# A four-layer graph network on one core: VectorE instead of GpSimd prepares each tile's edge rows in layer 0

## The reference, cut to what matters

```python
edge_index = jnp.stack([src, dst])            # 53125 edges among 3125 nodes, 256 features
x = _layernorm(x + _L0_gnn_ref(x, edge_index, W0, b0))       # layer 0
x = _layernorm(x + _L1_gnn_ref(x, edge_index, edge_weight, ...))
x = _layernorm(x + _L2_gnn_ref(x, W, att, src, dst))         # attention over edges
x = _layernorm(x + _L3_gnn_ref(x, edge_weight, W3, b3, src, dst))

# layer 0
h = x @ W
deg = segment_sum(ones, col, n)               # with a self loop for each node
dinv = rsqrt(deg)
out = relu(segment_sum(h[row] * (dinv[row] * dinv[col])[:, None], col, n) + b)
```

## Time and profile before

| | |
|---|---|
| median of 3 runs | 1625.72 us |
| lowest and highest run | 1624.23 and 1640.36 us |
| profiled execution | 1645.24 us |
| its span, first to last instruction | 1643.4 us |
| mean granted PE clock in it | 0.956 of full speed |
| busy: PE, DVE, POOL, ACT | 88%, 71%, 62%, 30% of the span |
| from 120 to 470 us, the steps of layer 0: PE busy | 326.66 of 350.00 us, clock 0.98 |
| same stretch: DVE busy, POOL busy | 276.90 and 267.95 us |
| same stretch: DMA engines busy | 0.49 of the time, 158 GB/s |

### The profile page before, as it was taken

One profiled execution on the slowest core, in us unless ns is written; L12 is line 12 of the kernel. 1 busy time (PEld: TensorE's weight loads), 2 busy tenths in 40 slices (PEclk: granted clock), 3 DMA queues, 4 the chain that ended last, 5 costly groups with the idle time before them and its releaser, 6 DMA issues.

```text
span 1643.4 us, 36677 instructions
## 1 busy us (share of the span) xinstructions
PE 1449.5 (88%) x12043; PEld 1159.1 (71%) x12043; DVE 1162.6 (71%) x2964; ACT 488.1 (30%) x909; POOL 1015.8 (62%) x1015
## 2 busy tenths in 40 slices
PE   4768899999888999999588888888888879999998
PEld 4657687778676788888366566666666657888887
DVE  9787878778683343445499999999999969444443
ACT  0332122212210010102345555555555546100000
POOL 0147777777773655655477777777777720357674
PEclk9989999999999999999699999989999979999999
DMA  8974554455467555552244444444444432666652
GB/s 205 104 153 148 167 162 133 161 173 165 129 207 246 185 190 171 183 176 68 72 113 112 112 114 113 112 112 113 113 112 112 113 111 99 246 216 214 208 155 79
DMA packets 132297, 241.50 MB, mean 147 GB/s; under 512 B 70299, under 2 KB 94975, under 8 KB 125967
## 3 DMA queue, kind: packets, MB, share of 16 engines
q0 software_dynamic: 45024, 128.68, 28.4%
q1 hardware_dynamic: 87087, 110.47, 22.5%
HBM read 193.42 MB, written 50.96 MB: 149 GB/s over the span
## 4 chain that ended last, share of the span: by engine, by line
PE 33%; POOL 29%; issue 18%; DVE 8%; DMA 8%; ACT 1%; POOLq 1%; SPq 0%; DVEq 0%; ACTq 0%
POOL ring L725 16%; PE bank L1718 15%; POOL ring L674 10%; PE bank L1666 7%; DMA ring<-edge_rows,ring 2%; PE bank L1850 2%; DMA big<-rows_layer,big 2%; POOL big L678 2%; PE bank L1727 2%; DMA ring<-rows_layer,ring 1%; DMA ring<-attention_rows,work 1%; PE bank L1536 1%; POOL ring L645 1%; PE bank L1501 1%; PE bank L1618 1%
## 5 line engine op out<-in xcount | busy, mean ns | idle before, releaser
L725 POOL DMA_INDIRECT ring<-attention_rows,work x420 | 398.5, 949 | 149.6 <-issue 147.2
L678 POOL DMA_INDIRECT big<-rows_layer,big x304 | 289.7, 953 | 265.4 <-issue 242.1
L674 POOL DMA_INDIRECT ring<-rows_layer,ring x152 | 233.2, 1534 | 54.2 <-issue 52.5
L1850 PE MATMUL bank<-work,ring 128*65 128x48 f32 x3360 | 238.8, 232 | 8.5 <-ACT work L890 7.9
L1850 PEld LDWEIGHTS bank<-work,ring 128*65 128x65 f32 x3360 | 227.9, 147 | 17.1 <-ACT work L890 14.4
L890 ACT ACTIVATE work<-work 128x960 f32<-128x960 f32 x84 | 161.6, 1924 | 84.2 <-DVE work L1397 83.2
L1718 PE MATMUL bank<-big,ring 128*128 128x256 f32 x750 | 164.2, 379 | 0.0
L1718 PEld LDWEIGHTS bank<-big,ring 128*128 128x128 f32 x750 | 142.5, 190 | 19.5
L1718 PE MATMUL bank<-big 128*128 128x256 f32 x664 | 145.9, 379 | 0.0
L1666 PE MATMUL bank<-big 128*128 128x256 f32 x608 | 139.8, 384 | 6.7 <-DMA big<-rows_layer,big 6.6
L1718 PEld LDWEIGHTS bank<-big 128*128 128x128 f32 x664 | 126.1, 190 | 17.7 <-ACT big L914 0.4
(11 more groups left out here) (256 smaller groups left out, 2343.6 us busy)
## 6 DMA issues: line engine op xcount, KB each, us to landing
adjacency<-big SPq DMA_DIRECT2D x16, 1600.0 KB, 6.6
big<-adjacency SPq DMA_DIRECT2D x16, 1600.0 KB, 7.6
ring<-adjacency SPq DMA_DIRECT2D x16, 1600.0 KB, 7.4
ring<-attention_rows,work POOLq DMA_INDIRECT x420
rows_layer<-big SPq DMA_DIRECT2D x50, 128.0 KB, 2.4
edge_rows<-edge_list SPq DMA_DIRECT2D x1, 4983.0 KB
big<-rows_layer,big POOLq DMA_INDIRECT x304, 3.0
rows_layer<-big SPq DMA_DIRECT2D x5, 960.0 KB, 10.5
```

The lines of the kernel that those rows point to most:

```text
L674: G.indirect_dma_start(out=rows0[:, s, :], out_offset=None, in_=y0tab[:, :], in_offset=bass.IndirectOffsetOnAxis(ap=src_l0[j][:, c:c + 1], ...
L678: G.indirect_dma_start(out=rows1[:, s, :], out_offset=None, in_=(y1tab if q < 2 * LAYER else y3tab)[:, :], in_offset=bass.IndirectOffsetOn ...
L725: G.indirect_dma_start(out=rows[0:EP, s, c, 0:ZG], out_offset=None, in_=ztab[:, :], in_offset=bass.IndirectOffsetOnAxis(ap=idx[:, g, c:c + ...
L1850: ins = mm(sum_banks[k % 3][0:FH, h * WIN:(h + 1) * WIN], rows[0:EP, s, c, h * FH:(h + 1) * FH], prob[:, k % 2, c, h * WIN:(h + 1) * WIN], ...
```

## The change

`edge_rows` on POOL keeps only the indirect DMA. The two small copies and the step of the row numbers become `next_rows` on DVE, and the panel test with the addition to `CODE` becomes `codes_of_panel` on DVE. In a step, DVE runs both between the second and the third `add_weights`: the codes of tile i+1, and the row numbers of tile i+2. The first ones stand ahead of the loop. The buffers `cur2` and `panel1` go.

```diff
-            pool.sem_inc(c_next, 1)
-
-            def edge_rows(col, i):
+
+            def edge_rows(i):
                 pool.wait_ge(c_T, i + 1)
                 pool.wait_ge(c_next, i + 1)
                 pool.sem_inc(held, 1)
-                G.tensor_copy(cur1, cur[:, bass.ds(col, 1)]).then_inc(pool_col, 1)
-                G.tensor_copy(panel1, panel[:, bass.ds(col, 1)]).then_inc(pool_col, 1)
-                pool.wait_ge(pool_col, 3 * i + 2)
-                pool.sem_inc(held, 1)
                 G.indirect_dma_start(out=raw.rearrange("p e f -> p (e f)"), out_offset=None, in_=etab[:, :],
                                      in_offset=bass.IndirectOffsetOnAxis(ap=cur1[:, 0:1], axis=0)).then_inc(c_gath, 16)
-                G.tensor_scalar(cur2, cur1, float(P // GRAN), float(DEAD), ALU.add, ALU.min).then_inc(pool_col, 1)
-                pool.wait_ge(pool_col, 3 * i + 3)
-                pool.sem_inc(held, 1)
-                G.tensor_copy(cur[:, bass.ds(col, 1)], cur2).then_inc(c_next, 1)
-                pool.wait_ge(c_gath, i * 16 + 16)
-                pool.sem_inc(held, 1)
-                G.tensor_scalar(off, raw[:, :, PID].bitcast(I16), panel1[:, 0:1], 256.0, ALU.is_equal,
-                                ALU.mult).then_inc(c_off, 1)
-                pool.wait_ge(c_off, i + 1)
-                G.tensor_tensor(raw[:, :, CODE], raw[:, :, CODE], off, ALU.add).then_inc(c_raw, 1)
...
+            def next_rows(i, col, first=False):
+                if not first:
+                    dve.wait_ge(c_gath, 16 * i)
+                    dve.wait_ge(c_moved, i)
+                V.tensor_scalar(cur1, cur[:, bass.ds(col, 1)], 0.0, None, ALU.add).then_inc(c_next, 1)
+                dve.wait_ge(c_next, i + 1)
+                V.tensor_scalar(cur[:, bass.ds(col, 1)], cur1, float(P // GRAN), float(DEAD), ALU.add,
+                                ALU.min).then_inc(c_moved, 1)
+
+            def codes_of_panel(i, col, first=False):
+                if not first:
+                    dve.wait_ge(c_raw, i)
+                dve.wait_ge(c_gath, 16 * i + 16)
+                V.tensor_scalar(off, raw[:, :, PID].bitcast(I16), panel[:, bass.ds(col, 1)], 256.0, ALU.is_equal,
+                                ALU.mult).then_inc(c_off, 1)
+                dve.wait_ge(c_off, i + 1)
+                V.tensor_tensor(raw[:, :, CODE], raw[:, :, CODE], off, ALU.add).then_inc(c_raw, 1)
...
             V.tensor_scalar(cur[:], first_f[:], float(DEAD), None, ALU.min).then_inc(s_cur, 1)
+            dve.wait_ge(s_cur, 1)
+            next_rows(0, DENSE[0], first=True)
...
+                if t == NT - 2:
+                    dve.wait_ge(s_nswb, 1)
+                    codes_of_panel(0, DENSE[0], first=True)
...
+            next_rows(1, (DENSE[0] + (nswb <= 1) * (DENSE[1] - DENSE[0])).with_bounds(min_val=DENSE[0], max_val=DENSE[1]))
...
-                        for q in range(4):
+                        for q in range(2):
+                            add_weights(k, i, q, r)
+                        codes_of_panel(i + 1, tile_of(k, r, 1))
+                        next_rows(i + 2, tile_of(k, r, 2))
+                        for q in range(2, 4):
                             add_weights(k, i, q, r)
```

More of the change, by code:

```diff
@@ L305, in gnn_program @@
         cur1 = carve(NPAN, 1, dt=I32)
-        cur2 = carve(NPAN, 1, dt=I32)
-        panel1 = carve(NPAN, 1)
         carve = carver(ring)
@@ L356, in gnn_program @@
         rows_landed = [sem(f"rows_landed{s}") for s in range(2 * TEN)]
-        rel_ready, hot_made, chunk_done, pool_col = sem("rel_ready"), sem("hot_made"), sem("chunk_done"), sem("pool_col")
+        rel_ready, hot_made, chunk_done, c_moved = sem("rel_ready"), sem("hot_made"), sem("chunk_done"), sem("c_moved")
         ld_dst, ld_src, ld_ew, ld_dsti, ld_x, ld_wts = (sem(f"ld_{n}") for n in ("dst", "src", "ew", "dsti", "x", "wts"))
@@ L683, in _ @@
                 G.memset(aw[j], 0.0).then_inc(c_zero, 1)
-            edge_rows(DENSE[0], 0)
+            edge_rows(0)
             for k in range(ND):
-                this, following = DENSE[k], DENSE[min(k + 1, ND - 1)]
                 with pool.Fori(0, nswb) as r:
-                    edge_rows((this + (r >= nswb - 1) * (following - this)).with_bounds(min_val=this, max_val=following)
-                              if following > this else this, nswb * k + r + 1)
+                    edge_rows(nswb * k + r + 1)
                 if k == 0:
@@ L1094, in _, with tile_of @@
             V.tensor_copy(unsorted[:], epsc[:]).then_inc(s_wz, 1)
-            dve.wait_ge(s_nswb, 1)
             nswb = dve.value_load(nswb_i[0:1, 0:1], min_val=1, max_val=MOST)
+            def tile_of(k, r, ahead):
+                this, following, then = (DENSE[min(k + j, ND - 1)] for j in range(3))
+                if then == this:
+                    return this
+                tile = this + (r + ahead >= nswb) * (following - this)
+                if ahead > 1:
+                    tile = tile + (r + ahead >= 2 * nswb) * (then - following)
+                return tile.with_bounds(min_val=this, max_val=then)
+            next_rows(1, (DENSE[0] + (nswb <= 1) * (DENSE[1] - DENSE[0])).with_bounds(min_val=DENSE[0], max_val=DENSE[1]))
             def one_hot_lo(h):
```

## The result

The changed kernel takes 1623.32 us (median of 20 runs, 1619.39 to 1627.50) against 1633.22 us (20 runs, 1622.28 to 1647.91). The ratio is 0.9937, 95% interval 0.9918 to 0.9956: faster by 0.6%, some 10 us, where the prediction said 24 us and 1601. The three runs of the kernel before that the prediction had to go by had a median of 1625.72 us, 7.5 us under that of the twenty. Note the spreads: 26 us before, 8 us after.

The account below looks back on a forecast made before the run. PE was taken to lose 26.6 us in layer 0's steps to rows gathered late by POOL. 26.6 - 5.6 + 0.9 + 3.2 - 0.9 = 24.2 us off the median 1625.72 gave 1601 us, range 1589 to 1618.

Parts of the forecast that it names:

- layer 0's waits are no longer for it, I take the microseconds off the median as they are: Whole kernel: the 24.2 us worked out on the profiled execution come off the median 1625.72 us in full, giving 1601.5.
- recovered by POOL: Layer 0's fourteen steps: all 26.6 us lost to late rows come back once POOL sheds its arithmetic, before what DVE adds.
- The floor of 308.0 us: Layer 0's fourteen steps with nothing waiting: seven at 20.71 us and seven at 23.29 us, against 334.59 us profiled.
- A stuck last gather is harmless: Ten-chunk steps: a last gather caught by DVE's run ends at 17.4 us; PE needs that row only 20.9 us in.
- The rule that spoke against the change: DVE's addition to `CODE` would be blocked by POOL's gathers, up to 15 us more over 16 steps; left out of the sum.
- DVE's insertion: Between second and third `add_weights`: 1.1 us of added work, making PE 0.4 us later a step, 5.6 us over fourteen steps.
- Rival A: DVE becomes the delay, registers unhidden and gathers met, 1.0 to 1.3 us a step: 1613 us, chance 0.11.
- B: Ten-chunk steps: the stall moves with the gathers and still gates PE, 10.5 us less gain: 1612 us, chance 0.10.
- C: DVE waits for edge rows landing after 7 us or more, stopping the quads: 11 us slower, 1637 us, chance 0.05.
- the low end: Of the range, 1589 us: DVE's lower bound (2.8 us more) and some 4 us for step 1's lower floor.
- Step 0: First step of layer 0: scatter's wait of 1.44 us goes, less 0.5 us for the insertion, 0.9 us gained.
- Step 15: Last step of layer 0: scatter waits and slow last matmuls recovered, less 0.4 us, some 3.2 us gained.

Follow-up runs that it names:

- b2_unchanged: The kernel before, unchanged, profiled again as a second further execution with its own trace: 1636.98 us in total, fourteen steps of 321.81 us.
- b3_unchanged: The kernel before, unchanged, profiled a third further time with its own trace: 1636.51 us in total, fourteen steps of 325.59 us.
- executions of the table: Six profiled executions without edits: four of the kernel before (1645.24, 1643.40, 1636.98, 1636.51 us) and two of the changed kernel (1622.16, 1627.93 us).
- e5_rows_late_again: Changed kernel with the row numbers moved two `add_weights` later, run again beside the changed kernel on one chip: 1616.15 us, against 1623.79 us.
- e2_rows_late: Changed kernel with the row numbers moved two `add_weights` later: 1620.90 us, ratio 0.9906 to the kernel before.
- b1: The kernel before, unchanged, profiled again as a first further execution with its own trace: 1643.40 us in total, fourteen steps of 334.02 us.

## Why the prediction was wrong

The forecast was a gain of 24.2 us and 1601 us; measured are 9.9 us and 1623.32.

**The step that failed** is "layer 0's waits are no longer for it, I take the microseconds off the median as they are". It carries the first term, 26.6 us "recovered by POOL", from one execution over to the median. For that execution the sum was nearly right: 1645.24 - 24.2 = 1621.0 us, and the changed kernel's profiled execution took 1622.16. But that execution had the longest steps of the four traced: 334.59 against 321.81 us of the shortest. With the latter the same working gives 321.81 - 308.0 = 13.8 us. I had seen that the profiled execution was 19.5 us over the three runs' median and put no place to it; a part of the very loss that the change removes was in it. By the traces, b2_unchanged and b3_unchanged reach layer 1 some 8 to 11 us after the changed kernel's two executions of the table, which is about the gain that was timed. Of the 21.8 us between 1601.5 and 1623.32, this transfer is 14.3; the other 7.5 are the median of three runs, which lay that much under the median of twenty. The surplus of the profiled execution should have been asked for first: in layer 0, three ten-chunk steps of the same work took 28.8, 28.8 and 23.3 us, so executions could differ there.

**What held.** The direction, and the mechanism: POOL's gathers start with PE's scatter, PE waits for none of them in the steps, and POOL waits for PE before each block, up to 11.2 us. The floor of 308.0 us: 307.70 with DVE's part removed, in part by luck as said above. A stuck last gather is harmless: a last gather still took 6.78 us in step 1 of the changed kernel, and in five of the fourteen steps of the one with late row numbers (e5_rows_late_again), and PE did not wait for a row. Four times in the changed kernel it was the gather of the edge rows that was held, for 6.7 us. The rule that spoke against the change (DVE's addition blocked by gathers that run beside it) is not seen: the 17 additions took 571 to 592 ns, the one at 98.45 us with no gather beside it and the one at 224.25 us with a gather that had started 0.67 us before it, both 0.57 to 0.58 us.

**DVE's insertion** was put at 1.1 us and took 1.26 in the median of the steps, PE's loss at 0.4 us a step and was 0.57 (8.0 us in fourteen steps in place of 5.6). Smaller terms were mis-sized here: behind the addition alone about 0.3 us of register work (0.58 us to the next operation, 0.30 in e2_rows_late), where 0.25 us was assumed for the whole, and a panel test of 0.29 us, in five steps 0.39 or 0.40, in place of 0.227. It lies within the bounds given. Rival A asked for 1.0 to 1.3 us a step, so it did not come about. B and C did not either; no row or edge row is waited for in the steps. The edge rows took 6.3 us to land in the median and 16.0 at most, where the forecast had 3 to 6 and C was to cost from 7 us on; yet DVE waited for them only once, 0.47 us at 114 us in step 0. Step 1, which relates no tile, took 21.5 us at the full clock (e2_rows_late), 1.8 under the floor of the other ten-chunk steps, where the low end allowed for 4.

**The ends.** Step 0: 116.01 to 134.99 is 18.98 us, where it had been 20.78: 1.8 gained in place of 0.9. Step 15: from the last transposes to layer 1 46.05 us, where it had been 48.22: 2.2 gained in place of 3.2. There a wait of 1.67 us for rows of the last block stays. Ahead of step 0's transposes 0.6 us were lost (116.01 against 115.41), in place of 0.9; since that point lay anywhere from 115.4 to 117.6 us in the executions of the table, it is no measurement. Nor are the other two: in b1, b2 and b3 step 0 took 19.2 to 19.9 us, and the stretch behind the last transposes 45.7, 50.0 and 45.8 us. The sum for the first two traces is 18.9 + 1.8 + 2.2 - 0.6 = 22.3 us at the start of layer 1.

**What stays open.** The medians of the kernel before were 1633.2, 1637.4, 1627.7 and 1635.6 us in four sets of runs, and single runs went down to 1614.85. All four traced executions took 1636.5 us or more, over the median of the first set. No trace shows what layer 0's steps look like in a median run or in the fastest; that fewer gathers get stuck in them is likely and not shown. Nor is it shown what decides whether a gather is held.

## What to carry to other kernels

A profile is one execution. Where the runs of a kernel spread by more than the effect that is to be sized, trace several executions before a wait's length becomes a term of a sum, and ask in which stage the spread lies. Before work is moved off an engine to shorten its stalls, find out what the stalls are: six added waits did in this case about what moving six instructions did. Before two sums over the same steps are compared, check the granted clock in both. And price an operation that is inserted between two waits of an engine with its register work; here the same operations cost less where longer ones ran just before them.

## What the runs showed of the hardware

A POOL gather that meets DVE's run of bf16 operations on SBUF, issued back to back, can be held until the run ends: 6.79 us, over some seven operations of about 1 us, not until the end of the one that is running. With waits added between these operations, it was let through within 2 us (1964 ns at most in 152); the two of the six that wait for the operation in front cost 0.12 us each, and the four satisfied ones no time that shows. The Trainium skill (SBUF — State Buffer, SBUF: two separate sides) says of the shared port pair that whichever starts first gets it "for the whole instruction", and that the other blocks. The trace agrees that the gather blocks; the length differs, it is a run of instructions and not one. And a run without added waits did let gathers through at times, as in b2_unchanged (1.50, 1.73, 1.50 us). It is not a matter of when in an operation the gather asks, as far as the traces resolve it: started 0.65 to 0.67 us after the beginning of the two products with which the run begins, 41 of 53 were held and 12 not. On what it depends, no run here settles.
